# Second attention: the SyncE list reordered around the key loads, and the router's exponentials moved by one tick

## The reference

```python
qkv = (x @ w_qkv).reshape(B, T, 3, H, hd)          # H = 8 heads of 32
scores = q @ k.T * scale, causal; scores += head_scales * q_proj * k_proj
x = layernorm(x + softmax(scores) @ v @ w_out)
xn = rmsnorm(x) * norm_weight
probs = softmax(xn @ router_weight.T + router_bias) # 16 experts
gate_vals, expert_idx = top_k(probs, 2)             # places in experts by rank, 512 at most
x = layernorm(x + combine(experts(dispatch(xn))))
```

## Time and profile before

| what | value |
|---|---|
| median of 3 runs | 1966.1 us (1964.29 to 1966.22) |
| profiled execution | 1972.85 us, its span 1971.1 us |
| mean granted TensorE clock | 0.945 |
| busy: PE, DVE, ACT, POOL | 1813.4, 1428.9, 1124.2, 510.7 us |
| second attention, line 2693 | from 1166.0 to 1577.6 us of the span |

### The profile page before, as it was taken

One profiled execution on the slowest core, in us unless ns is written; L12 is line 12 of the kernel. 1 busy time (PEld: TensorE's weight loads), 2 busy tenths in 40 slices (PEclk: granted clock), 3 DMA queues, 4 the chain that ended last, 5 costly groups with the idle time before them and its releaser, 6 DMA issues. The chain is left out here.

```text
span 1971.1 us, 34758 instructions
## 1 busy us (share of the span) xinstructions
PE 1813.4 (92%) x12676; PEld 1181.2 (60%) x12676; DVE 1428.9 (72%) x2803; ACT 1124.2 (57%) x2228; POOL 510.7 (26%) x648
## 2 busy tenths in 40 slices
PE   8979999999999999799999869898999868899992
PEld 4545444444444444688888745564555457899992
DVE  7869999999999996467766555565656454566663
ACT  4635888888888889323222215454544523655554
POOL 5750000332000001223221122114324243344441
PEclk9976999999999999899999969989989989999996
DMA  4883734654353302115434454646545253555645
GB/s 168 289 239 46 116 82 93 143 137 127 62 82 72 63 19 82 41 52 176 136 107 132 154 141 110 140 94 165 125 127 135 69 164 109 136 141 145 157 91 184
DMA packets 169717, 238.99 MB, mean 121 GB/s; under 512 B 25689, under 2 KB 109178, under 8 KB 169568
## 3 DMA queue, kind: packets, MB, share of 16 engines
q1 hardware_dynamic: 138256, 178.82, 37.1%
q0 software_dynamic: 15200, 26.76, 5.8%
q10 hardware_dynamic: 16112, 31.46, 4.5%
HBM read 136.97 MB, written 96.60 MB: 118 GB/s over the span
## 5 line engine op out<-in xcount | busy, mean ns | idle before, releaser
L988 DVE TENSOR_REDUCE b_mx<-b_PM 128x1 f32<-128x512 f32 x1024 | 621.1, 683 | 22.3 <-PE b_PM L842 21.9
L964 ACT ACTIVATE b_probs<-b_PS 128x512 f32<-128x512 f32 x1000 | 523.9, 606 | 69.0 <-PE b_PS L896 53.5
L2781 ACT ACTIVATE d_probs<-d_PS 128x512 f32<-128x512 f32 (+3 forms) x384 | 166.7, 496 | 202.7 <-PE d_PS L2693 202.1
L842 PE MATMUL b_PM<-b_kst,b_qst 48*128 48x512 f32 x888 | 281.4, 431 | 0.0
L2821 DVE TENSOR_REDUCE d_mx<-d_PM 128x2 f32<-128x1024 f32 (+1 forms) x192 | 180.1, 951 | 114.9 <-PE d_PM L2645 68.7
L896 PE MATMUL b_PS<-b_qst,b_kst 50*128 50x512 f32 x744 | 257.0, 437 | 1.8
L896 PEld LDWEIGHTS b_PS<-b_qst,b_kst 50*128 50x128 f32 x744 | 120.5, 184 | 163.4 <-ACT b_probs L964 147.8
L2744 POOL TENSOR_SCALAR_AFFINE_SELECT d_probs<-d_probs 128x128 f32<-128x128 f32 x256 | 77.7, 317 | 271.5 <-ACT d_probs L2781 267.1
L868 PE MATMUL b_PO<-b_probs,x_v 128*32 128x384 f32 (+2 forms) x2048 | 145.2, 390 | 0.0
L842 PEld LDWEIGHTS b_PM<-b_kst,b_qst 48*128 48x128 f32 x888 | 142.1, 185 | 5.3
L868 PE MATMUL b_PO<-b_probs,b_vst 128*32 128x384 f32 (+3 forms) x1960 | 143.0, 397 | 1.0 <-ACT b_probs L964 0.9
(11 more groups left out here) (300 smaller groups left out, 3761.8 us busy)
## 6 DMA issues: line engine op xcount, KB each, us to landing
halves<-a_parts SPq DMA_DIRECT2D x7, 2048.0 KB, 8.7
qk<-c_halves ACTq DMA_DIRECT2D x7, 2048.0 KB, 12.4
w_w<-L_ffn_fc1T SPq DMA_DIRECT2D x12, 1024.0 KB, 4.9
w_w<-L_ffn_fc2T SPq DMA_DIRECT2D x12, 1024.0 KB, 6.4
b_qst<-halves SPq DMA_DIRECT2D x72, 128.0 KB, 4.4
b_kst<-halves SPq DMA_DIRECT2D x72, 128.0 KB, 7.6
d_qst<-qk SPq DMA_DIRECT2D x36, 256.0 KB, 4.7
d_kst<-qk SPq DMA_DIRECT2D x36, 256.0 KB, 6.9
```

Of the source, the lines that this page charges most:

```text
L842: mm = pe.matmul(PM[n % MBANKS][:], qst[buf][at, p, first:first + P], kst[buf][at, p, kh * BLK:(kh + 1) * BLK], start=True, stop=True)
L964: act.activation(probs[:, s % RING], score_bank(g, s)[:], ACT.Exp).then_inc(exped, 1)
L988: dve.tensor_reduce(mx[:, half, (r * PAIRS0 + p) * TPH + t, kh:kh + 1], PM[n % MBANKS][:], AX.X, ALU.max)\
L2781: act.activation(probs[:, s % RING, 0:w], PS[bank(s)][:, 0:w], ACT.Exp).then_inc(exped, 1)
```

## The change

Three edits. In the SyncE list of the second attention `load(g + 3)` goes in front of `load_shares(g - 1, 1)` and `store_shares(g, 0)`. The stores of the normed tokens go from the third group of a batch to the end of the fourth. The router's exponentials go from k = 29 to k = 30 on ScalarE, and on VectorE the three operations that need them (sum, reciprocal, product), which were at k = 30 and 31, are all at k = 31.

```diff
-    LOGITS, EXPS, RANKS = 27, 29, 39
+    LOGITS, EXPS, RANKS = 27, 30, 39
...
-    LAST_ACT = {24: (20,), 25: (22,), 26: (23,), 30: (24,), EXPS + BEHIND: (29,)}
+    LAST_ACT = {24: (20,), 25: (22,), 26: (23,), 30: (24,), EXPS + BEHIND: (30,)}
...
-        if k == self.LOGITS + 3:
+        if k == self.EXPS + 1:
             dve.wait_ge(self.expd_done, u + 1)
             dve.tensor_reduce(self.total[:, us], self.expd[:, us], AX.X, ALU.add).then_inc(step, 1)
             past(4)
             dve.reciprocal(self.rtotal[:, us], self.total[:, us]).then_inc(step, 1)
-        if k == self.LOGITS + 4:
             past(5)
             dve.tensor_tensor(self.prob[:, us], self.expd[:, us], tiles(self.rtotal[:, us]), ALU.mult).then_inc(step, 1)
...
                 if g + 1 < GROUPS:
                     rows(g + 1)
+                if g + BUFS - 1 < GROUPS:
+                    if g > 0:
+
+                        sp.wait_ge(pv_done, g * ROUNDS + RING // G1)
+                    load(g + BUFS - 1)
                 if g > 0:
                     route.load_shares(sp, d, g - 1, 1)
                 route.store_shares(sp, d, g, 0)
-                if g + BUFS - 1 < GROUPS:
-                    if g > 0:
-
-                        sp.wait_ge(pv_done, g * ROUNDS + RING // G1)
-                    load(g + BUFS - 1)
+                b = g // HG1
                 if g % HG1 == HG1 - 2:
-                    b = g // HG1
                     route.load_tokens(sp, d, b)
-                    if b > 0:
-
-                        for n in range((b - 1) * HPS, b * HPS):
-                            tokens.store(sp, d, n)
+                if g % HG1 == HG1 - 1 and b > 0:
+
+                    for n in range((b - 1) * HPS, b * HPS):
+                        tokens.store(sp, d, n)
```

More of the change, by code:

```diff
@@ L2597, in _ @@
                     rows(g + 1)
-                if g > 0:
-                    route.load_shares(sp, d, g - 1, 1)
-                route.store_shares(sp, d, g, 0)
                 if g + BUFS - 1 < GROUPS:
@@ L2605, in _ @@
                     load(g + BUFS - 1)
+                if g > 0:
+                    route.load_shares(sp, d, g - 1, 1)
+                route.store_shares(sp, d, g, 0)
+                b = g // HG1
                 if g % HG1 == HG1 - 2:
-                    b = g // HG1
                     route.load_tokens(sp, d, b)
-                    if b > 0:
-                        for n in range((b - 1) * HPS, b * HPS):
-                            tokens.store(sp, d, n)
+                if g % HG1 == HG1 - 1 and b > 0:
+                    for n in range((b - 1) * HPS, b * HPS):
+                        tokens.store(sp, d, n)
             route.load_shares(sp, d, GROUPS - 1, 0)
```

## The result

The change makes the kernel slower. The median is 1979.47 us (1976.15 to 1982.89, 7 runs) against 1966.1 us (7 runs of the kernel before beside them): ratio 1.0067, 95% interval [1.0053, 1.008], 13.4 us. I had predicted 1960, with 1942 to 1970 as the range; the sign is wrong and the time lies outside. The profiled execution took 1978.04 us.

A forecast was written before the change was run, and what follows sets the result against it. TensorE sets the pace in quiet groups, waits reaching it in the others. 11 + 13 + 3 - 20 - 1 = 6 us gain from 1966.1 gave 1960; range 1942 to 1970 for 8 in 10.

The forecast's parts named there:

- By the same 4.6 us per MB these come some 2 us late for VectorE: Second totals of groups 7 and 11, behind 3 MB with the moved stores: 2 us late for VectorE.
- the cover: At those second totals, VectorE's slack and two tiles of maxima absorb the 2 us; only SyncE's later list is pushed back.
- Keys in front: Key loads issued 5.9 us earlier in group 4: TensorE's key waits and their clock loss go, 11 us gain.
- The rival by which the keys are bound by the queue's rate: Key loads: 9 of the 11 us are not gained, sum 3 us slower, 1969; chance 0.1.
- Stores: Stores one group later: VectorE's totals waits in groups 7 and 11 go, with their clock loss, 13 us gain.
- Exponentials: Router's exponentials a tick later: ScalarE's wait in groups 6, 10 and 14 goes, 3 us gain (0.5 to 5).
- Shares of the second half: Load behind 2 MB of keys and values, late for `weigh` in groups 5, 9, 13: 20 us loss (0 to 33).
- Tail: Last stores move from group 14 to 15, delaying the last shares' load: 1 us loss (0 to 2.5).
- 27 of gain against 21 of loss: Whole kernel: gains 11, 13 and 3 us, losses 20 and 1 us, sum 6 us gain.
- The new wait takes everything back: Rival: second block's `weigh` in groups 5, 9, 13 loses 11 us each; 7 us slower, 1973; chance 0.2.
- The shares are in time: Rival: second half's shares reach `weigh` nearly in time, loss 0 to 4 us; 24 us faster, 1942; chance 0.12.

The follow-up runs named there:

- late_stores: The change, with the stores of the normed tokens in groups 9 and 13 and batch 2's in the tail; 1969.2 us, ratio 1.0017.
- combined2: late_stores, with the second half's shares loaded in front of the keys only in groups 4, 8 and 12; 1952.9 us, ratio 0.9921.
- before_again: The kernel before, unchanged, run again for noise and a second profile; 1967.44 us, ratio 0.9996.
- combined: shares_first, with the stores of the normed tokens in groups 9 and 13 and the last two batches' in the tail; 1968.7 us, ratio 0.9978.
- keys_only: The kernel before, with only the key loads moved in front of the shares; 1975.34 us, ratio 1.0039.
- shares_first: The change, with the load of the second half's shares in front of the keys again; 1975.13 us, ratio 1.0006.
- shares_on_act: The change, with the load of the second half's shares issued on ScalarE's queue at tick 9; 1973.64 us, ratio 0.9997.
- before_third: The kernel before, unchanged, one execution for a later profile; 1966.03 us.

## Why the prediction was wrong

**The step that failed is "By the same 4.6 us per MB these come some 2 us late for VectorE"**, with the cover that followed from it. It is the term for the second totals of groups 7 and 11, with keys, values and stores in front of them: 3 MB were to take 13.8 us and took 20.6. VectorE waited 7.43 and 7.66 us, too much for its slack, and tick 9 of groups 8 and 12 grew by 13.8 us, where I had put 0 and only carried 2 us on. The 6.8 us that were missing have three parts. 3 MB took 15.2 us in the kernel before itself (group 3), since the time is not in proportion to the MB: 12.2, 15.2 and 18.6 us for 2, 3 and 4. With the keys in front 3 MB took 18.6 us, without a scatter: the keys start earlier, but the totals behind them come no earlier by as much. And in group 8, with scatters, they took 20.6. Why the second arises was not taken apart (SyncE was held 7.60 us at the tokens there), and no run took the scatters away.

**A term was missing beside it: the shares of the first half.** `store_shares(g, 0)`, and with it the load that waits for it, was also moved behind the keys. I had followed only `load_shares(g - 1, 1)` past the 2 MB. In the change this wait is partly hidden behind the one for totals: VectorE waits 2.15 us for these shares in group 4, where the tick is 3.8 us longer, and 1.74 and 1.47 in groups 8 and 12, in the same tick 9. So the 13.8 us are not the stores' alone. In late_stores and combined2 the stores are gone from there and VectorE's totals waits are down to 3.3 to 3.7 us, and ticks 9 and 10 of groups 8 and 12 are still 11.6 and 11.3 us longer, now behind waits of 3.1 to 3.4 us at `weigh`, which in three of the four places the view puts down to these shares (in group 12 of combined2 to the sums). What was gained at the keys in groups 4, 8 and 12 (12.5 us) is waited for again a few ticks later: `weigh` of the first block starts 19.3 us into group 8 in before_again and 19.0 us in late_stores. In combined it is the other way round: the key ticks of these groups are 5.1 us longer than in the base, and ticks 9 and 10 are not longer at all. No run gave the first half's shares a place of their own, so their price apart from the keys is not known. "Every instruction behind a moved block is late by it" would have led me here.

**Keys in front: the waits went.** 11 us forecast. The key waits fell from 9.3 to 0.8 us in keys_only, and the ticks there are 14.6 us shorter in the change, against before_again; against the other two profiles of the kernel before it is 9 and 11. Groups 1 to 3 became 0.7 to 1.5 us shorter than in the first profile, for 0.7 to 0.9 foreseen. The rival by which the keys are bound by the queue's rate falls with this, as it had said itself.

**Stores: 13 us of gain forecast, none found.** Alone they gave nothing (0.4 us slower, interval 3.7 us faster to 2.4 slower). With the keys in front, the kernel is at 1.0067 with their move and at 1.005 without. Groups 7 and 11 did give 11.3 us, but 9.7 of them come with the keys' move (keys_only): the same wait can be removed only once. That the 11.3 is near the 13 is luck. I had the totals of group 7 come 9.6 us earlier; counted from the group's start, they come at 14.5 us instead of 18.5, 4.0 earlier, just enough to leave a wait of 1.04 us. The edits don't add either: 8.7, 0.4 and -4.1 us alone make 5, together they make 13 to 17. Even keys and exponentials, which share no wait that I know of, make 4.6 alone and 10.2 together, in different sets; so some of this may be the sets.

**Exponentials: right.** 3 us forecast, 4.1 measured alone, inside the 0.5 to 5 given.

**Shares of the second half: right in place and mechanism, near in size.** 20 us forecast; 15.6 in the traces, and 16.3 by combined2 against late_stores, of which their profiles show 9.1 in these ticks. VectorE's new waits are 1.21, 3.90 and 3.35 us, TensorE's 2.97, 5.66 and 5.10 for 1.66 before. The clock follows as I had put it: 0.50 for 4 us behind the second of them. shares_first shows that the place in the list decides: the same load in front of the keys, and groups 5, 9 and 13 are at 26.5 us. The Trainium skill (DMA: Bandwidth & Descriptors, Queues, rings and completion order) says that on each DMA engine descriptors are consumed in ring order. The trace agrees with it: the values, issued in front of the shares at 1382.49, landed after 9.1 us, and VectorE had the shares at 1393.84, 2.3 us behind them. A queue of its own did not help the load in group 8 of shares_on_act, where it took 11.0 us.

**Tail.** 1 us forecast. VectorE's wait for the last shares went from 9.87 to 12.36 us; the part behind the attention took 396.3 and 397.9 us in the two profiles of the change, 393.8 to 395.6 in those of before. That is 1 to 4 us, seen only in profiles and tried by no run of its own.

**The sum in one line.** I had 27 of gain against 21 of loss. The ticks of the change show 25.9 of gain (14.6 at the keys, 11.3 in groups 7 and 11), to which the router may add up to 2, against 15.6, 14.0 and 3.8 of loss and about 1 in the tail. That leaves 6 to 9 us of loss, where the two spans differ by 9.9 and the medians by 13.4; the rest I can't place. Only the 14.0 and the 3.8 stood at 0 or were missing in my list, and they make the sign.

**The rivals.** "The new wait takes everything back" had the right sign and the wrong place: it needed 8.7 us in each of groups 5, 9 and 13 and there are 5.2. The loss that decided lies one group earlier, in one wait that I had declared covered and one that I had not looked for. "The shares are in time" is refuted by VectorE's row at 1393.84.

## What to carry to other kernels

How long a small load takes behind large ones is not a rate times their MB: here 2, 3 and 4 MB took 12.2, 15.2 and 18.6 us in one order of the list and 14.7, 18.6 and 21.2 in another. Before using such a time in another stage, look there for the same sequence of issue and landing, and for what else is on the DMA engines. Where a large transfer is moved forward in a queue, list all that was ahead of it and when each is needed, small loads and stores with loads chained to them included, and let only the one with a near due time stay in front. Edits that shorten the same wait have one gain between them. And where one wait on a path is removed, look for the next one that the engine will now reach early: it can take the gain back.

## What the runs showed of the hardware

- A load of 128 KB issued directly behind 2 MB of the same queue was used 10.6 to 10.9 us after its issue (groups 5, 9 and 13 of the change). Put in front in these three places it made the kernel 16.3 us faster by the medians (some 5 us of uncertainty), 8.1 us in the attention of the two profiles. Issued on ScalarE's queue beside the same keys it took 11.0 us too, in group 8 of shares_on_act.
- In group 8, 3 MB took 20.6 us until the totals behind them were used, with scatters on queue 0 (24% of the DMA engines); in group 7 of the same kernel, without them, 18.6.
- The issue of two 512 KB stores held SyncE for 5.84 us in the kernel before and for 7.84 us in the one after, where keys, values and scatters were under way; the issue of two 512 KB token loads held it for 1.13 us and, behind keys and shares, for 7.60. All that SyncE issues behind them is late by this too.
- Two profiles of one kernel differ by 6.8 us in span (1971.1, and 1964.3 in before_third), and all of it is in the attention (411.1 and 404.3), mostly in a few groups: 28.2 and 26.5 us in group 5, 30.7 and 28.4 in group 6, 28.2 and 26.5 in group 13 (group 10 goes the other way, 28.5 and 31.0). The one that I predicted from was the slower.
- Combined2, 12.8 us faster than the kernel before, still has VectorE waiting 3.3 us for totals and 3.2 us for shares of the first half in group 8. A separate place for these in front of the keys wasn't tried.
